# Masked row maxima of a latent attention: the mask added by VectorE in the instruction that takes the extremum, in place of TensorE products into PSUM

## The reference, cut to what matters

```python
c_kv = x_kv @ W_kv_down.T
c_sel = c_kv[jnp.arange(b)[:, None, None], indices]
kv = (c_sel @ W_kv_up.T).reshape(b, nq, K, 2, H, HD)
scores = jnp.einsum('bqhd,bqkhd->bqkh', q, k) * SCALE
attn = jax.nn.softmax(scores, axis=2)
out = jnp.einsum('bqkh,bqkhd->bqhd', attn, v).reshape(b, nq, d)
return out @ W_out.T
```

## Time and profile before

| | us |
|---|---|
| median of 3 runs (lowest, highest) | 3688.69 (3685.52, 3695.85) |
| the profiled execution | 3701.36 |
| its span in the trace | 3699.6 |
| PE busy | 3146.5 (85%) |
| DVE busy | 2772.8 (75%) |
| ACT busy | 2089.9 (56%) |
| POOL busy | 923.8 (25%) |

### The profile page before, as it was taken

How to read it: one execution, slowest core, us unless ns; L and a number is a source line. 1 busy time by engine, 2 the same in 40 slices (tenths; PEclk the granted TensorE clock), 3 DMA queues, 4 the chain that set the end, 5 groups by cost and what they waited for, 6 DMA issues and landing times.

```text
span 3699.6 us, 59631 instructions
## 1 busy us (share of the span) xinstructions
PE 3146.5 (85%) x22658; PEld 2231.3 (60%) x22658; DVE 2772.8 (75%) x4915; ACT 2089.9 (56%) x4816; POOL 923.8 (25%) x740
## 2 busy tenths in 40 slices
PE   2568989898898989889898988989899898989877
PEld 1245656666565666656666665666666566666555
DVE  4677796878779697877969778796877879687522
ACT  2346656565665656556565655656565565656332
POOL 1414041231404123140412314031231503223000
PEclk8679999999999999999999999999999999999988
DMA  5212141421314142231413213141321414132110
GB/s 190 87 50 87 40 153 53 140 83 65 125 48 156 53 138 84 68 120 49 155 53 136 86 54 135 49 153 56 136 87 46 143 49 153 56 128 88 53 39 18
DMA packets 208286, 338.71 MB, mean 92 GB/s; under 512 B 24480, under 2 KB 177568, under 8 KB 193280
## 3 DMA queue, kind: packets, MB, share of 16 engines
q1 hardware_dynamic: 208000, 334.90, 26.5%
HBM read 311.75 MB, written 20.97 MB: 90 GB/s over the span
## 4 chain that ended last, share of the span: by engine, by line
PE 55%; DVE 27%; ACT 12%; issue 5%; POOL 0%; SPq 0%; DMA 0%; DVEq 0%; ACTq 0%
PE ps L636 6%; DVE nm L1567 6%; PE ps L888 4%; PE ps L617 3%; PE ps L754 3%; PE ps L848 3%; PE ps L834 3%; PE ps L803 3%; PE ps L869 3%; PE ps L789 3%; PE ps L779 3%; PE ps L556 3%; PE ps L648 2%; DVE region_x L1544 2%; DVE rmax L1672 2%
## 5 line engine op out<-in xcount | busy, mean ns | idle before, releaser
L1331 POOL TENSOR_TENSOR region_x<-region_x 128x512 f32<-128x512 f32 x512 | 645.3, 1274 | 249.9 <-DVE region_x L1544 247.8
L1544 DVE TENSOR_TENSOR_SCAN region_x<-ps,region_x 128x512 f32<-128x512 f32 x512 | 615.5, 1213 | 56.8 <-ACT ps L1070 54.3
L1070 ACT ACTIVATE ps<-region_x,aneg 128x255 f32<-128x255 f32 x1024 | 441.8, 471 | 299.3 <-DVE region_x L1544 173.2
L1311 POOL TENSOR_TENSOR region_x<-region_x 128x512 f32<-128x512 f32 x96 | 121.8, 1268 | 1210.5 <-ACT region_x L1018 1205.5
L1323 POOL TENSOR_TENSOR region_x<-region_x 128x512 f32<-128x512 f32 x128 | 162.4, 1269 | 996.2 <-DVE region_x L1524 734.3
L1567 DVE TENSOR_REDUCE nm<-ps 128x4 f32<-128x1024 f32 x256 | 307.5, 1222 | 47.3 <-PE ps L617 41.8
L888 PE MATMUL ps<-xTy,wide 128*128 128x256 f32 x1280 | 318.0, 399 | 1.6 <-DVE region_y L1731 1.4
L1219 ACT ACTIVATE region_y<-ps,rmax 128x256 f32<-128x256 f32 x512 | 236.0, 494 | 104.4 <-DVE rmax L1672 104.4
L1524 DVE TENSOR_TENSOR region_x<-region_x,ps 128x512 f32<-128x512 f32 x384 | 254.3, 666 | 17.3 <-PE ps L556 16.6
L888 PEld LDWEIGHTS ps<-xTy,wide 128*128 128x128 f32 x1280 | 245.1, 198 | 36.2 <-DVE region_y L1731 1.7
L1111 ACT ACTIVATE region_y<-ps 128x512 f32<-128x512 f32 x256 | 142.8, 594 | 218.3 <-PE ps L636 218.3
(11 more groups left out here) (251 smaller groups left out, 6765.6 us busy)
## 6 DMA issues: line engine op xcount, KB each, us to landing
region_x<-rows_of_dt SPq DMA_DIRECT2D x1024, 128.0 KB, 2.9
wide<-in_wgate SPq DMA_DIRECT2D x16, 1280.0 KB, 8.4
wide<-in_wup SPq DMA_DIRECT2D x16, 1280.0 KB, 11.1
down<-in_wmoe SPq DMA_DIRECT2D x16, 1280.0 KB, 5.5
wide<-in_wq SPq DMA_DIRECT2D x16, 1024.0 KB, 6.2
wide<-in_wk SPq DMA_DIRECT2D x16, 1024.0 KB, 8.2
wide<-in_wv SPq DMA_DIRECT2D x16, 1024.0 KB, 10.7
down<-in_wo SPq DMA_DIRECT2D x16, 1024.0 KB, 13.7
```

The source lines that it names most:

```text
L1070: last = f(ps[:, 1 + 2 * (k % 2), half * T + 1:(half + 1) * T], dt_rep[k % SLOTS][:, 1:T], ACT.Exp, scale=aneg[:, k, half:half + 1])
L1331: nc.gpsimd.tensor_tensor(hbuf[k % HSLOTS], hbuf[k % HSLOTS], csb, ALU.mult).then_inc(hc_ready, 1)
L1544: nc.vector.tensor_tensor_scan(flat(hbuf[k % HSLOTS]), ps[:, 1 + 2 * (k % 2), :], flat(hbuf[k % HSLOTS]), 0.0, ALU.mult, ALU.add).then_inc ...
```

## The change

The four mask products of each latent unit go, and with them PE's waits for the mask. The score products start their own accumulation. DVE's one `tensor_reduce` per latent unit becomes four `tensor_tensor_reduce`: each reads 256 score elements of a PSUM bank and 256 bf16 elements of the mask, adds them, multiplies by -1, writes the 256 results to a scratch part of `region_x` that nobody reads, and keeps the minimum in a column of `nm`. Each of them is two instructions on the engine, the second of which writes the accumulated minimum. `mask_other`, its two DMAs per sequence and their semaphore go, and the identity shrinks to 128 columns.

```diff
                     if k == 12:
                         yield
-                        sp.wait_ge(cnt_max, i + 1)
-                        for half in (0, 64):
-                            sp.dma_start(mask_other[64 - half:P - half], mask[half:half + 64]).then_inc(mask_turned, 16)
...
                     if u >= 2:
                         pe.wait_ge(a.rmax, at(i, 8, u - 1))
-                    if a.masked:
-                        pe.wait_ge(cnt_max, i + 1)
-                        pe.wait_ge(mask_turned, at(i, 32, 32))
-                        for own in (True, False):
-                            for j in range(2):
-                                r = slice(64 * j, 64 * j + 64)
-                                rows, first = (mask, 0) if own else (mask_other, 64)
-                                mm(ps[:, b + j, :], W["identb"][r, first:first + P], rows[r].rearrange("p q k -> p (q k)"),
-                                   start=own, stop=False)
                     for qt in range(TT):
                         for j in range(2):
                             r = slice(64 * j, 64 * j + 64)
                             last = mm(ps[:, b + j, qt * T:(qt + 1) * T], a.QT[r, t, qt * P:(qt + 1) * P], a.KT[u % 2][r, t, :],
-                                      start=not a.masked, stop=not a.masked or qt == TT - 1)
+                                      start=True, stop=True)
...
                     v.wait_ge(a.s_ps, at(i, 8, u + 1))
-                    last = nc.vector.tensor_reduce(at_nm[:, u % 2::2, :, 16 + t],
-                                                   ps[:, b:b + 2, :].rearrange("p g (q k) -> p g q k", k=T),
-                                                   AX, ALU.max, negate=True)
+                    if a.masked:
+                        for j in range(2):
+                            for qt in range(TT):
+                                column = 32 * (2 * j + u % 2) + 16 + t
+                                last = nc.vector.tensor_tensor_reduce(
+                                    a.junk[:, 4 * (u % 2) + 2 * j + qt], ps[:, b + j, qt * T:(qt + 1) * T], mask[:, qt], -1.0, -MASKED,
+                                    ALU.add, ALU.min, a.NM[:, qt, column:column + 1])
+                    else:
+                        last = nc.vector.tensor_reduce(at_nm[:, u % 2::2, :, 16 + t],
+                                                       ps[:, b:b + 2, :].rearrange("p g (q k) -> p g q k", k=T),
+                                                       AX, ALU.max, negate=True)
                     last.then_inc(a.rmax, 1)
```

More of the change, by code:

```diff
@@ L105 @@
     ("wdt", (RANK + 2 * NS, DI), F32), ("bdt", (P, M), F32), ("dp", (P, M), F32),
-    ("ident", (P, P), F32), ("identb", (P, P + 64), BF16), ("ones", (P, P), F32),
+    ("ident", (P, P), F32), ("identb", (P, P), BF16), ("ones", (P, P), F32),
     ("iota", (P, 32), BF16), ("half", (P, 1), F32), ("sely", (P, 2, 32), F32),
@@ L151, in build @@
         cntk = sb("cntk", (P, TT, T), BF16)
-        mask, mask_other = sb("mask", (P, TT, T), BF16), sb("mask_other", (P, TT, T), BF16)
+        mask = sb("mask", (P, TT, T), BF16)
         VP0, VP1 = sb("VP0", (P, TT, VW)), sb("VP1", (P, TT, VW))
@@ L270, in build @@
             sem("gate_ps"), sem("up_ps"), sem("w_ps"), sem("gu_silu"), sem("moe_t"), sem("moe_h"))
-        batch_done, mask_turned = sem("batch_done"), sem("mask_turned")
+        batch_done = sem("batch_done")
         b_sb, dbx_pool = sem("b_sb"), sem("dbx_pool")
@@ L499, in counts_by_key @@
                     for kt in range(TT):
-                        last = tr(keys[:, kt, qt * P:(qt + 1) * P], cntq[:, qt, kt * P:(kt + 1) * P], W["identb"][:, 0:P])
+                        last = tr(keys[:, kt, qt * P:(qt + 1) * P], cntq[:, qt, kt * P:(kt + 1) * P], W["identb"][:])
                 last.then_inc(cntk_ps, 1)
@@ L695, in ffn @@
                     for k in range(KD):
-                        last = tr(psb[:, k, tt * P:(tt + 1) * P], qb[:, tt, k * P:(k + 1) * P], W["identb"][:, 0:P])
+                        last = tr(psb[:, k, tt * P:(tt + 1) * P], qb[:, tt, k * P:(k + 1) * P], W["identb"][:])
                 last.then_inc(f_qT_ps, 1)
@@ L726, in ffn @@
                         last = tr(ps[:, b, :].bitcast(BF16).rearrange("p (k t) -> p k t", t=P)[:, k, :],
-                                  qb[:, tt, k * P:(k + 1) * P], W["identb"][:, 0:P])
+                                  qb[:, tt, k * P:(k + 1) * P], W["identb"][:])
                     last.then_inc(f_qT_ps, 1)
@@ L821, in cross_attention @@
                 for qt in range(TT):
-                    last = tr(turned_shift[:, qt * P:(qt + 1) * P], shiftb[:, qt, :], W["identb"][:, 0:P])
+                    last = tr(turned_shift[:, qt * P:(qt + 1) * P], shiftb[:, qt, :], W["identb"][:])
                 last.then_inc(a.shift_ps, 1)
@@ L910, in moe @@
                 for tt in range(TT):
-                    last = tr(ps[:, 4, 0:P].bitcast(BF16)[:, tt * P:(tt + 1) * P], wsplit[:, tt, :], W["identb"][:, 0:P])
+                    last = tr(ps[:, 4, 0:P].bitcast(BF16)[:, tt * P:(tt + 1) * P], wsplit[:, tt, :], W["identb"][:])
                 last.then_inc(wT_ps, 1)
@@ L1846, in layouts @@
         "bdt": columns(n["L0_attn_b_dt"]), "alog": by_unit(n["L0_attn_A_log"]), "dp": columns(n["L0_attn_Dp"]),
-        "ident": np.eye(P, dtype=np.float32), "identb": np.tile(np.eye(P, dtype=np.float32), 2)[:, 0:P + 64].astype(bf),
+        "ident": np.eye(P, dtype=np.float32), "identb": np.eye(P, dtype=np.float32).astype(bf),
         "iota": np.tile(np.arange(32, dtype=np.float32), (P, 1)).astype(bf),
```

## The result

| | before | changed |
|---|---|---|
| median, us (runs) | 3691.67 (4) | 3726.14 (4) |
| lowest, highest | 3685.52, 3695.85 | 3725.68, 3729.37 |
| span of the profiled execution | 3699.6 | 3724.0 |
| mean granted clock there | 0.953 | 0.945 |

The ratio is 1.0089, 95% interval 1.0069 to 1.0110: the change costs 0.9%, 33 us by the ratio and 34 by the medians, where the forecast was 1.5%, 55 us. A second set of six runs, beside eleven of the kernel before, gave 1.0079 (1.0057 to 1.0102). The direction and the place were right; the size was not.

What follows compares the result with a forecast made beforehand. DVE was taken to bound the latent stage, hiding most of PE's saving. +53.3 us over fifteen sequences and +1.9 in sequence 0 made +55.2 on 3688.7: 3743.9 us, taken as 3744, range 3725 to 3795.

Steps and rivals of the forecast that it cites:

- What bounds the kernel: Latent stage, 13.05 us: DVE is waited for, so PE's saving is hidden except at each sequence's last unit.
- What comes: DVE, per latent unit: four add-and-minimum pairs at 0.41 us replace one reduction, 1.65 per unit with hand-over.
- lower bound: DVE's pair at best: 0.33 us main part plus a read-out like a tiny instruction, 0.06, together 0.39.
- 3.40: Fixed us per sequence in the latent stage: two cross units 2.26, shift 1.01, hand-over 0.05, last instruction's end 0.08.
- The rival of 0.48 to 0.56: DVE's read-out drains the pipe: 0.48 us per pair, +90 us, or 0.56, +131 us; chance 0.13.
- The clock: PE's clock dips behind the latent stage, about 1.7 us per sequence, +26 us over fifteen, 3770; chance 0.15.
- PE is late for no unit: Latent stage: PE needs 0.86 us per unit, 1.16 where it has waited, both below DVE's 1.65.
- Sequence 0: The sequence without a second stream: its eight latent units go from 10.92 to 12.85 us, +1.9.
- The sum: Latent stages: +3.55 us in each of fifteen sequences, +53.3, and +1.9 in sequence 0, together +55.2 us.
- Two cycles per element: DVE's main part runs at the scan's rate: pair 0.66 to 0.67 us, +187 us, 3876; chance 0.06.
- two elements per cycle: DVE's custom addition at double rate: pair 0.27 us, -19 us, 3670; not slower 0.05, of which faster 0.03.
- Delay given back later: Behind the latent stage: the forecast gave nothing back; delay partly absorbed, under +30 us but slower, had chance 0.03.

Runs made afterwards that it cites:

- experiment 2: The changed kernel with the DVE edit undone: no mask products, plain maximum by one reduction per latent unit; 3681.40 us, ratio 0.9970 to the kernel before.
- experiment 6: The kernel before with DVE's add-and-minimum in all latent units and PE's mask products dropped in unit 7 alone; 3713.22 us, ratio 1.0048.
- experiment 7: The changed kernel run again, 3726.37 us; and with a write of 512 zeros on DVE before the addition to the queries, ratio 1.0089.
- Experiments 1: The kernel before with PE's mask products kept and DVE's add-and-minimum put in as well; 3729.94 us, ratio 1.0096.

## Why the prediction was wrong, point by point

**What bounds the kernel.** Right. The stage is DVE's, and what PE saves there is hidden but for the last unit: experiment 2 gave 13.20 for the 13.2 that follows from the forecast's arithmetic.

**What comes: the step that failed.** The term of the sum that was mis-sized is the price of the pair. The forecast took 0.41 (0.33 for the main part, 0.07 for the read-out, 0.01 of margin), and its lower bound was 0.39. It is 0.344: 0.332 for the main part and 0.012 for the minimum with its read-out. With 8 x 0.344 x 4 + 3.40 the forecast's own sum gives 14.41 against 13.05, +1.36 per sequence; measured without the clock's fall, 14.88 - 13.61 = +1.27. Over fifteen sequences 19.1 us in place of 53.3. The error was made at the lower bound. I took the distance of two tiny instructions as the least that any further instruction can cost, when ACT's rows already showed 0.05, below that bound, and I added a margin toward the bad end where the row pointed the other way. The rival of 0.48 to 0.56 came from the Trainium skill's rule on the emptying pipeline ("VectorE: DVE Perf Modes", The DRAIN you can't avoid). The row of the read-out at 596.12 contradicts it: the main part in front ends at 596.20, and the next one starts at 596.12 too. The same section of the Trainium skill adds that a next instruction that isn't held starts earlier, which the prediction did not take up; the row agrees with that.

**The clock: the second step that failed.** The rival was real and was priced in the wrong place. I expected a fall behind the stage at 1.7 us per sequence, gave it 0.15, and left the forecast without it; and I wrote that PE is late for no unit. The clock falls in the stage, and there PE is late for the last one (DVE waits 0.59). DVE covers part of it: the fall costs 0.68 in each sequence of the first trace (15.56 - 14.88), 1.63 in four of the second. That it is the clock, and nothing in the products, is shown by experiment 6 and by the two windows of experiment 7. Experiments 1 and 6 have more PE work and no fall in any stage, in one trace each. What decides in which sequences it comes isn't shown: in the changed kernel's second trace a stage with PE busy for 10.41 of 14.88 us kept its clock, and in its first trace none did.

**Sequence 0.** Forecast +1.9. With 0.344 the same working gives about -0.3. Measured, the addition to the queries came at 176.74, and at 176.97 before the change.

**The sum.** 19.1 for DVE, 6.5 to 10.2 for the clock in the stage, -0.2 for sequence 0: 25 to 29 us. The two ratios say 29 and 33 us. The remaining few us are not settled. They are of the size of the spread outside the stages, 3016.1 and 3035.2 in two traces of the kernel before, 3030.7 and 3032.9 in two of the changed one. That the total came as near to the forecast as it did is in part luck: the clock, which the forecast left out, made up for some of the pair's price, which it had too high.

**The other rivals.** Two cycles per element would have made a pair 0.66, two elements per cycle 0.27; both are refuted by the 0.344. Delay given back later: the spans of the first traces differ by 24.4 where the stages grew by 29.2, those of the second by 41.2 where they grew by 25.6, so nothing is seen to be given back beyond the spread.

## What to carry to other kernels

Where two engines are level, price the move on the engine that the chain of waits runs over in that stage; the shares over the whole span (85% and 75% here) pointed the other way. On DVE, count distances from start to start: here an add with a running minimum and its accumulator read cost 0.344 where the add alone cost 0.332. And before making a mask cheaper, ask whether the result needs it: here the softmax's shift doesn't.

## What the runs showed of the hardware that was not expected

- A read-out of DVE's accumulator (0.08 long) and the next custom instruction start at the same recorded time; from the two sizes measured, 128 and 256 elements (0.211 and 0.344), the pair costs 1.04 ns per element and 0.08 us fixed.
- With 48 us of products that add a mask which DVE adds again, the kernel was no slower, by its medians 13 us faster (3713 against 3726). PE's clock stayed at its upper level in all its latent stages, which is 6.5 to 10.2 us of it.
- In one kernel, with the same instructions, a sequence takes 216.25 to 221.1 us, and the places at which PE's clock falls differ with it. The kernel before spreads from 3681 to 3713 us over its runs; in two traces of it the difference went with these falls. A change of ten microseconds can't be read from one trace of each kernel, but it can from a stage that repeats to 0.02 us while its clock is full.
